# Edge attention by stretches per tile, in one loop with the edge counting

## The reference, cut to what matters

```
h = einsum('ni,hio->hno', x, W)                       # 4 heads of 64
e = attn_src[:, src] + attn_dst[:, dst]
e = where(e >= 0, e, 0.2 * e) * edge_weight
e_exp = exp(e - max(e))
denom = segment_sum(e_exp, dst)
out = segment_sum(h[:, src] * e_exp / denom[:, dst], dst)
```

## Time and profile before

| | us |
|---|---|
| median of three runs (5355.04 to 5360.88) | 5360.76 |
| profiled execution, its own time | 5351.66 |
| its span, first to last instruction | 5350.0 |
| TensorE busy in the span (79%) | 4206.0 |
| VectorE busy (45%) | 2415.1 |
| ScalarE busy (37%) | 1956.5 |
| GpSimd busy (16%) | 838.3 |
| mean granted clock of TensorE | 0.871 |

### The profile page before, as it was taken

The page is one execution under the profiler, slowest core; times in us unless marked ns, Lnnn a source line. Parts: engine busy times, 40 slices in busy tenths (PEclk is TensorE's granted clock), DMA queues, the critical chain, the costliest instruction groups (busy, mean ns, idle before and its releaser), DMA issues. The chain is left out here.

```text
span 5350.0 us, 78843 instructions
## 1 busy us (share of the span) xinstructions
PE 4206.0 (79%) x23793; PEld 3714.3 (69%) x23794; DVE 2415.1 (45%) x4124; ACT 1956.5 (37%) x3059; POOL 838.3 (16%) x777
## 2 busy tenths in 40 slices
PE   3788856883649969694997998997599779699576
PEld 2677746772539945583886887886499779699454
DVE  3555558765350030215995895897411230110423
ACT  2333304661320033233664665665143310210422
POOL 2777730000520000220000000000122200000001
PEclk8788877885879989897998998998699989899788
DMA  3433325991333310321110110110222233133000
GB/s 101 114 113 110 105 60 113 171 172 29 110 111 153 138 32 0 111 87 58 55 58 29 59 58 34 50 57 29 84 69 69 80 114 153 62 149 148 10 18 26
DMA packets 235159, 441.37 MB, mean 82 GB/s; under 512 B 113420, under 2 KB 177633, under 8 KB 218544
## 3 DMA queue, kind: packets, MB, share of 16 engines
q1 hardware_dynamic: 199888, 343.13, 21.2%
q0 software_dynamic: 35168, 97.06, 6.4%
HBM read 343.76 MB, written 96.35 MB: 82 GB/s over the span
## 5 line engine op out<-in xcount | busy, mean ns | idle before, releaser
L2471 PE MATMUL p_acc<-p_H,p_eT 125*125 125x256 f32 x3750 | 823.9, 379 | 0.0
L2471 PEld LDWEIGHTS p_acc<-p_H,p_eT 125*125 125x125 f32 x3750 | 696.4, 187 | 105.2
L1100 POOL DMA_INDIRECT p_message<-edge_table,p_index x425 | 499.4, 1175 | 132.2 <-issue 120.6
L2018 DVE TENSOR_REDUCE p_mean<-F 128x1 f32<-128x3125 f32 x10 | 34.0, 3403 | 932.0 <-PEq L90 932.0
L1313 PE MATMUL p_acc<-p_message,p_spread 125*125 125x260 f32 x1666 | 422.7, 420 | 28.7 <-issue 28.7
L1772 ACT ACTIVATE p_hid<-p_up,p_b1s 128x125 f32<-128x125 f32 x764 | 272.1, 365 | 396.3 <-PE p_up L1748 352.6
L1313 PEld LDWEIGHTS p_acc<-p_message,p_spread 125*125 125x125 f32 x1666 | 346.2, 210 | 97.3 <-issue 30.6
L1748 PEld LDWEIGHTS p_up<-p_xT,p_w1s 128*128 128x128 f32 x3056 | 373.8, 198 | 50.3 <-issue 33.1
L1748 PE MATMUL p_up<-p_xT,p_w1s 128*128 128x125 f32 x3056 | 381.3, 282 | 32.3 <-issue 10.8
L1756 PE MATMUL p_down<-p_w2s,p_hid 128*125 128x256 f32 x1528 | 360.2, 385 | 12.1 <-ACT p_hid L1772 11.2
L497 PE MATMUL p_turned<-identity,p_slot 125*128 125x125 f32 x400 | 88.4, 376 | 310.4 <-DVE p_slot L465 306.8
(11 more groups left out here) (469 smaller groups left out, 6959.8 us busy)
## 6 DMA issues: line engine op xcount, KB each, us to landing
sums_first<-edge_sums SPq DMA_DIRECT2D x48, 1250.0 KB
p_second<-edge_sums SPq DMA_DIRECT2D x48, 1250.0 KB, 6.7
p_count<-edge_counts SPq DMA_DIRECT2D x75, 762.9 KB
edge_sums<-p_sums SPq DMA_DIRECT2D x32, 1250.0 KB, 4.8
edge_counts<-p_total SPq DMA_DIRECT2D x32, 546.9 KB
p_w1s<-in_L_ffn_W SPq DMA_DIRECT2D x16, 1024.0 KB
p_got<-made SPq DMA_DIRECT2D x25, 560.0 KB
p_dst_all<-dst_row SPq DMA_DIRECT2D x25, 531.2 KB, 4.3
```

The source lines that it names most:

```text
L1100: pool.indirect_dma_start(message[:, m, k, :], None, table, bass.IndirectOffsetOnAxis(ap=index[:, m, k:k + 1], axis=0)).then_inc(landed[m] ...
L2018: then(dve.tensor_reduce(mean[:, h:h + 1], F[:, h], AX_X, ALU.add))
L2471: last = pe.matmul(acc[:, s, 0:C], eT[:, r % 4, a % 4], H[:, a, 0:C], start=(a == 0), stop=(a == T - 1))
```

## The change

Attention goes by tile, as the counting does by unit. For each tile of 125 destinations the edges begin at a known place of the sorted list; the new `load_units` finds it and gathers 18 stretches of 128 edges from there (2304 places for at most 2206 edges of a tile here; edges of other tiles get a penalty that makes their exponent zero). A tile is therefore visited once, with 18 matmuls, and its total needs no rescaling. The counting uses groups of 125 destinations (25 units, in six sets of four and one of one), so a tile and a group are the same 125 nodes, and both kinds of work stand in one loop over tiles, `edges_by_units`. Its stores go from `XT`, which is free then. `attend_rest` is a new stage: a loop for tiles with more than 18 stretches, which runs at least once, and the closing division by the sums. `load_graph` loads only `x`.

```diff
-GD = 100
-GROUPS = -(-N // GD)
+GD = P
+GROUPS = N // GD
...
-            with eng.Fori(0, PAIRS // 2) as i:
-                for m in range(2):
-                    one(i * 2 + m, i, m)
+            with eng.Fori(0, PAIRS // 2) as i:
+                for m in range(2):
+                    one(i * 2 + m, i, m, 2)
+            one(PAIRS, PAIRS // 2, 0, 1)
...
-                attend_edges(nc, g, edge_table, a_dst, d["dst_flat"], dst_row, X)
-            with ExitStack() as st:
                 units = Units(nc, st)
                 load_units(nc, g, units, d["ends"], d["windows"])
-                count_edges(nc, g, units, counts, weights)
+                total = st.enter_context(nc.sbuf_tensor("total", [P, T, C + HEADS], F32))
+                peak = st.enter_context(nc.sbuf_tensor("peak", [128, T], F32))
+                edges_by_units(nc, g, units, edge_table, a_dst, d["dst_flat"], counts, weights, total, peak, XT)
+                attend_rest(nc, g, units, edge_table, a_dst, d["windows"], d["dst_flat"], total, peak, X)
                 count_rest(nc, g, units, counts, weights, d["windows"])
```

More of the change, by code:

```diff
@@ L166, in __init__ @@
         self.ones = sb("ones", [128, P])
[L168 to L175, removed]
@@ L178, in tile_at @@
[L178 to L188, removed]
@@ L278, in _ @@
[L278 to L285, removed]
+            dve.memset(g.ones[:], 1.0)
@@ new lines, in __init__ @@
+        self.row = sb("rows", [128, 2, SPLIT + 1])
+        self.value = sb("value", [128, 2, UNITS], BF16)
+        self.part = sb("part", [128, PARTS_OF, UNITS], BF16)
+        self.all_ones = sb("all_ones", [128, 128])
+        self.four = sb("four", [128, HERE, QK], BF16)
+        self.shifted = sb("shifted", [128, 256], BF16)
+        self.own = sb("own", [128, UB + 1, T], BF16)
+        self.edges = sb("edges", [128, 3, SLOTS_OF])
+        self.index = sb("index", [128, T * WK], I32)
+        self.penalty = sb("penalty", [128, T * WK])
@@ L340, in _, with rows_below @@
-            for m in range(SPLIT):
-                rows_below(0, m)
-                dve.tensor_copy(index[:, m:m + 1], units.row[:, 0, m:m + 1]).then_inc(indexed, 1)
-            for m in range(SPLIT):
-                rows_below(1, m)
+            def rows_below(m):
+                then(dve.tensor_scalar(below[:], ends_all[:], bound[:, m:m + 1], 0.0, ALU.is_lt, ALU.add, accum_out=units.row[:, 0, m:m + 1]))
+            rows_below(SPLIT)
+            dve.sem_inc(tile_rows_ready, 1)
+            rows_below(0)
@@ L682, in _ @@
                 one(i * 2 + 1, 1)
+            one(PAIRS, 0, 1)
         @block.tensor
@@ L762, in _ @@
             then = Steps(dve, setup)
-            src, dst, weight = (units.edges[:, f] for f in range(3))
-            then(dve.tensor_scalar(scaled[:], src, 4195.0, None, ALU.mult))
-            then(dve.tensor_copy(hi_i[:], scaled[:]))
-            then(dve.tensor_scalar(hi_i[:], hi_i[:], 19, None, ALU.arith_shift_right))
-            then(dve.tensor_copy(hi[:], hi_i[:]))
-            then(dve.scalar_tensor_tensor(out=value[:, 0], in0=hi[:], scalar=-float(P), in1=src, op0=ALU.mult, op1=ALU.add))
@@ new lines, in _ @@
+            logits(0)
+            tops(0)
+            peaks(0)
+            for s in range(NP):
+                scales(0, s)
+                spreads(0, s)
+            for t in range(T):
+                coming = t + 1 < T
[13 more added lines that the diff above has]
+                    marks(t, 3 + s)
```

1000 lines of the change are left out of this document (524 added, 476 removed).

## The result

| | before | after |
|---|---|---|
| median, us (least to most) | 5358.81 (5355.04 to 5360.88) | 5209.69 (5208.85 to 5211.48) |
| ratio after / before, 95% interval | | 0.9723 [0.9706, 0.9740] |
| span of the profiled execution | 5350.0 | 5207.1 |

A forecast was written before the change was run, and what follows sets the result against it. It took POOL to pace attention, with no engine full in attention or counting. Terms of -6, +1, -149 (merged stage 919 us for 1068.2), +43 and -20 sum to -131: 5351.7 - 131 = 5221 us, range 5140 to 5340.

The forecast's parts named there:

- Around the merged stage: Other stages: first stage -6 us, unit loading +1, attention's new remainder pass +43, three aggregations -20.
- First turn, 23 turns, last tile: Merged tile loop: 79 us, 23 x 34.9 = 803, and 37 with the stores; together 919 us.
- What paces the turn: Merged loop: a 34.9 us chain of TensorE's burst and DVE's list, DVE standing still about 9 us a tile.
- The burst: TensorE's 18 visits a tile: 36 passes at 0.22 us plus about 10 cold passes, 10.0 us.
- POOL is covered: Merged loop: POOL's gathers, 22.5 us a tile or near 29 with hold-ups, fit beside the chain and cost nothing.
- marks: DVE's marks in the merged loop: 0.69 + 0.96 us and links of 0.2, 1.86 us a set.
- the one-unit set: Last set of a tile's marks on DVE: a quarter of the elements, 1.15 us beside 5.58 for three sets.
- Links: Added between steps of the turn: eight of 0.08 us in scalings and spreads, 0.2 us in a set's marks.
- The hold-up of gathers: POOL's gathers wait for the running two-SBUF-input DVE operation to end, 0.5 us on average, perhaps for three quarters of them.
- The cold burst: Rival, TensorE's burst: all 36 passes at 0.45 us, 16.2 for 10.0, +140 us, 5361 in all; chance 0.10.
- The warm burst: Rival, TensorE's burst: starts at full clock, 7.9 us for 10.0, 5173 in all; chance 0.10.
- DVE does not stand still: Rival, merged loop: marks 1 and 2 fill DVE's wait, POOL paces at 29 us a tile, -136, 5085; chance 0.04.

The follow-up runs named there:

- e_order: On the change: the next maximum's transposition and spread issued inside TensorE's burst, ScalarE's exponents ahead of its copies; 5107.2 us, ratio 0.9562.
- e_apart: The change with the merging undone: attention over 25 tiles in one loop, then counting in another, same instructions; 5302.3 us, ratio 0.9925.
- e_warm: On e_align: 12 unread bf16 matmuls on zeros after sets 3, 4 and 5 of each tile, ahead of the burst; 5146.1 us, ratio 0.9602.
- e_queue: On e_both: the load of a tile's destinations issued one turn earlier, ahead of the stores; 5052.9 us, ratio 0.9425.
- e_both: On the change: the edits of e_align and e_order together; 5101.0 us, ratio 0.9553.
- e_align: On the change: value and weight tables laid out with 26 columns a tile in place of 25; 5167.0 us, ratio 0.9672.

## Why the prediction was right

The forecast of 5221 us missed by 11 us, where the change was worth 149; its steps in turn:

- **Around the merged stage** -6, +1, +43 and -20 were foreseen; -7.2, +0.8, +42.2 and, for the stages of the three aggregations, -18 came.
- **First turn, 23 turns, last tile**: 79, 803 and 37 foreseen; 74.9 to the second burst, 23 x 34.34 = 789.9, and 40.2 from the last burst on. The stage came 14 us under the 919 foreseen, most of it from the 23 turns.
- **What paces the turn.** PE's burst, then DVE's list, with DVE idle behind the burst: foreseen at 9 us a tile, 8.3 measured, and ended by PE's transposition. e_order shows that this idle time is on the path: taking most of it away gave 104 us.
- **The burst.** 10.0 us with 8 to 12 slow passes foreseen; 9.2 to 10.4 with 6 and 11.
- **POOL is covered.** It was: it waited 142 us for visits. The mean gather was 1.146 us, below the 1.2 to 1.5 that the text named as a sign. The DMA engines had more to do than foreseen, 0.75 x 905 / 25 = 27 us a tile for 23, and were covered too.
- **The gain is the overlap**, so far as 96 of 163 us go (e_apart); 27 of the others only moved to other stages.

But the turn of 34.9 us is right only as a sum, and no single turn had it. Set beside the two turns of the timeline above, in us:

| step | foreseen | even tile | odd tile |
|---|---|---|---|
| burst | 10.0 | 9.2 | 10.3 |
| set 0, transposition, maximum | 2.6 | 2.4 | 2.4 |
| marks 1, then products to the minus, marks 2 | 6.0 | 5.7 | 7.0 |
| four scalings and spreads | 9.1 | 7.7 | 7.7 |
| three sets of marks | 5.58 | 4.8 | 6.8 |
| the one-unit set | 1.15 | 1.6 | 1.6 |
| last unit on PE | 0.5 | 0.6 | 0.6 |
| turn | 34.9 | 31.9 | 36.4 |

Two terms of the sum were mis-sized, and that they nearly cancel is luck. *Links* of 0.08 to 0.2 us were added between DVE's operations; in fact a scaling, a spread or a first mark starts before the operation ahead of it has ended, so marks take 1.6 and not 1.86 us a set, and scalings and spreads 7.7 and not 9.1. The price of *marks* was taken from the earlier trace rows, where a group of 20 units begins at an even element for every batch; with 25 units a tile half of the tiles begin at an odd one. Five sets a tile lie on the path, 0.67 us each: 3.3 of the 4.5 us between neighbouring turns; the rest is the burst. The one-unit set was taken by its elements; its operations of 384 and 256 elements took 1.02 and 0.72 us, as much as the whole ones of even tiles.

**The hold-up of gathers.** That a gather waits for the end of the one DVE operation that runs is seen again in the timeline of POOL and DVE of the changed kernel:

```profile
570.61 0.95 POOL L800 DMA_INDIRECT p_message<-edge_table,unit_index  x1 [0.30 <-issue]
570.65 1.36 DVE L939 TENSOR_TENSOR p_heavy<-p_cell,unit_part 128x1536 bf16<-128x1536 bf16 x1
...
575.43 1.36 DVE L939 TENSOR_TENSOR p_heavy<-p_cell,unit_part 128x1536 bf16<-128x1536 bf16 x1
...
575.63 1.97 POOL L800 DMA_INDIRECT p_message<-edge_table,unit_index  x1 [0.30 <-issue]
```

The gather at 575.63 began inside a mark that ended at 576.79, and was done at 577.60, 0.81 later; the one at 570.61 began 0.04 us before a mark and took its 0.95 us. The Trainium skill ("SBUF — State Buffer", Who interferes with whom) says, of VectorE's modes that take both ports, that whoever issues first gets the ports shared with GpSimd for the whole instruction and that the other waits. Both rows agree with that order, here for marks with two inputs in SBUF. It is no matter of two rows: of the 450 gathers 213 began inside a mark, a scaling or a spread, and the median one of them ended 0.82 us after it. What the forecast had too high is how often a gather loses time: 184 of 450 took over 1.0 us, 1.44 in the mean. That is the half microsecond foreseen, for two gathers of five and not for three of four.

**The rivals.** The cold burst did not come. The warm burst would have been worth 48 us by the forecast; e_warm made it, and got 23 in the stage. "DVE does not stand still" was put at 29 us a tile, paced by POOL; e_queue, where that is so, has 27.5 in the mean.

## What to carry to other kernels

Where two engines run in order and hand work to each other, look for the engine that waits behind a burst, and move the small steps of the next round into the burst; then look again, since the next bound may be a load that stands behind a store in one queue and cost nothing before. A slice of two-byte elements that starts at an odd index makes VectorE's operation about 1.4 times as long here, and padding each block to an even length cost nothing that could be seen. VectorE's instructions that follow each other without a wait overlap in this trace, by 0.08 us after a scaling and 0.20 after a mark of one unit: price a list by start-to-start times, not by durations and links.

## What was not expected of the hardware

- The two levels of the marks by the parity of their first element: 0.68 and 0.94 us for 1024 elements, 0.96 and 1.36 for 1536.
- The one-unit set, whose elements lie in runs of one, is dear: 384 elements took 1.02 us, 1536 in runs of four 0.96. It took as long in odd tiles as in even ones. That the runs are the reason was not tried.
- The store of a tile's counts held SP's queue for 6.88 us in the turn shown (6.4 to 9.4 over the stage of e_both), and a load behind it in the list went out after it.
- The bursts' slow passes come as 6 and 11 in turn in the change, and in e_align too, where all turns have the same work (turns of 31.9 and 33.0). Why they alternate was not tried.
